# Experts in two groups of tokens with half tiles of 128 rows, and the scatters gathered behind the last attention unit

## What is computed

```python
x = _L0_conv_ref(x, ...)                      # softmax attention over 1024 positions, 4 images
t = _to_tokens(x)                             # (4, 1024, 128)
t = t + _L1_attn_ref(_ln_t(t), ...)
t = t + _L1_ffn_ref(_ln_t(t), ...)

def _L1_ffn_ref(x, Wg, bg, W1, b1, W2, b2):
    gate_logits = xf @ Wg + bg                # xf: (4096, 128), 8 experts
    top_w, top_i = jax.lax.top_k(gate_logits, 2)
    top_w = jax.nn.softmax(top_w, axis=-1)
    for e in range(E):
        h = jax.nn.gelu(xf @ W1[e] + b1[e], approximate=False)     # 512 hidden
        out = out + w_dense[:, e:e + 1] * (h @ W2[e] + b2[e])
```

## Time and profile before

| | us |
|---|---|
| median of 3 runs | 542.87 |
| lowest, highest | 540.98, 543.97 |
| profiled execution, its own time | 542.02 |
| its span, first to last instruction | 540.1 |
| TensorE busy | 397.8 (74%) |
| VectorE busy | 403.1 (75%) |
| GpSimd busy | 339.8 (63%) |
| ScalarE busy | 291.1 (54%) |

### The profile page before, as it was taken

The page is one execution under the profiler, slowest core; times in us unless marked ns, Lnnn a source line. Parts: engine busy times, 40 slices in busy tenths (PEclk is TensorE's granted clock), DMA queues, the critical chain, the costliest instruction groups (busy, mean ns, idle before and its releaser), DMA issues.

```text
span 540.1 us, 13443 instructions
## 1 busy us (share of the span) xinstructions
PE 397.8 (74%) x3902; PEld 294.2 (54%) x3903; DVE 403.1 (75%) x1119; ACT 291.1 (54%) x567; POOL 339.8 (63%) x361
## 2 busy tenths in 40 slices
PE   3767689999797998999884483001989898989336
PEld 2433356666575665666654362000778797979212
DVE  2578979988886878898878766700688898989457
ACT  3537887887675997776663123200545455555102
POOL 8000336567997558887599777773087878778800
PEclk9878999999998999999997597555899999999855
DMA  5730004200000000000620111332223323232176
GB/s 195 182 54 1 0 1 94 66 3 1 1 0 2 1 2 1 2 1 1 140 77 10 55 51 51 89 94 59 51 75 85 85 83 88 77 91 76 44 249 227
DMA packets 44244, 33.30 MB, mean 62 GB/s; under 512 B 17702, under 2 KB 37161, under 8 KB 44201
## 3 DMA queue, kind: packets, MB, share of 16 engines
q1 hardware_dynamic: 39594, 23.24, 17.1%
q0 software_dynamic: 4608, 9.51, 5.3%
HBM read 18.98 MB, written 13.73 MB: 61 GB/s over the span
## 4 chain that ended last, share of the span: by engine, by line
POOL 27%; PE 25%; DVE 20%; issue 17%; ACT 6%; DMA 3%; POOLq 0%; ACTq 0%; SPq 0%; DVEq 0%
POOL zbuf L503 12%; POOL ybuf L606 9%; PE PV L618 7%; PE SC L618 7%; PE MX L618 6%; DVE mx L1303 5%; PE PR L618 4%; DVE EL L1326 4%; POOL EL L544 2%; ACT EH L1032 2%; DVE TOK L1579 2%; ACT QK L950 2%; DVE QK L1271 1%; POOL carry L604 1%; DVE TOK L1584 1%
## 5 line engine op out<-in xcount | busy, mean ns | idle before, releaser
L544 POOL TENSOR_TENSOR EL<-E,EH 128x1024 f32 (+1 forms) x31 | 67.0, 2160 | 58.2 <-ACT EH L1032 58.2
L1031 ACT ACTIVATE E<-SC 128x512 f32<-128x512 f32 x128 | 77.2, 603 | 48.0 <-PE SC L618 34.1
L618 PE MATMUL PV<-VH,EH 128*128 128x129 f16 x512 | 97.2, 227 | 2.4 <-DVE TOK L1346 1.9
L606 POOL DMA_INDIRECT ybuf<-QK,yid x80 | 87.1, 1089 | 18.3 <-issue 12.5
L618 PE MATMUL SC<-QK 128*128 128x512 f16 x320 | 90.5, 386 | 9.9 <-ACT EH L1032 7.2
L618 PE MATMUL PV<-VH,EL 128*128 128x129 f16 x512 | 96.8, 224 | 0.0
L618 PE MATMUL PV<-VL,EH 128*128 128x128 f16 x512 | 96.7, 222 | 0.0
L1303 DVE TENSOR_REDUCE mx<-MX 128x1 f32<-128x1024 f32 x64 | 78.0, 1218 | 20.2 <-PE MX L618 19.9
L1032 ACT ACTIVATE EH<-SC 128x512 f32 (+1 forms) x128 | 77.5, 605 | 0.0
L503 POOL DMA_INDIRECT zbuf<-ZZ,posi x64 | 65.4, 1022 | 18.9 <-issue 18.9
L618 PE MATMUL MX<-EL,EH 128*128 x640 | 59.4, 246 | 1.6 <-DVE QK L1536 1.6
(11 more groups left out here) (200 smaller groups left out, 860.4 us busy)
## 6 DMA issues: line engine op xcount, KB each, us to landing
EH<-zbuf SPq DMA_DIRECT2D x40, 130.0 KB, 2.2
X<-in_x_dram SPq DMA_DIRECT2D x4, 512.0 KB, 5.1
zbuf<-zer SPq DMA_DIRECT2D x16, 128.0 KB, 3.3
X<-in_L_ffn_W_dram SPq DMA_DIRECT2D x1, 2048.0 KB
EL<-ybuf SPq DMA_DIRECT2D x4, 512.0 KB, 5.6
EH<-ybuf SPq DMA_DIRECT2D x4, 512.0 KB, 8.9
out_dram<-X SPq DMA_DIRECT2D x8, 256.0 KB, 2.7
ybuf<-QK,yid POOLq DMA_INDIRECT x80, 2.3
```

The lines of the kernel that those rows point to most:

```text
L544: nc.gpsimd.tensor_tensor(EL[:, w % 2, ds(i * 2, 2), c], E32h[1], EH[:, w % 2, ds(i * 2, 2), c], ALU.subtract).then_inc(e32_free[1], 1)
L606: nc.gpsimd.indirect_dma_start(out=ybuf, out_offset=bass.IndirectOffsetOnAxis(ap=yid[:, b, q:q + 1], axis=0), in_=y32[:, b, q, :], in_offs ...
L618: return nc.tensor.matmul(o, w, r, start=start, stop=stop)
L1031: nc.scalar.activation(E32h[h][:, p, :], SC[:, p, :], ACT.Exp, scale=sc)
```

## The change

- **Two groups.** Images 0 and 1 are group 0, images 2 and 3 group 1 (`G`, `GB`). Each has its own region in `zbuf` and its own tile table; `tile_table(0)` comes after the second image's `place`, `tile_table(1)` after the last. SyncE waits for a group's 32 scatters alone, then loads its 20 tiles; the pads of group 1 stand behind the load of tile 19 in its queue. TensorE's loop waits for both tables.
- **Half tiles.** A half tile has 128 rows (`TR`) and its own expert; two of them make a tile of the loop, still 256 rows, still 40 tiles. Loads are two to a tile. `hidden` and `output` run per half, with 128-column matmuls throughout: 24 and 26 instead of 12 and 16. b2 is added by one matmul a half (ones times a row of `B2`), which is prepared in the first steps by two DMAs, two ScalarE copies and one VectorE operation.
- **Output.** VectorE scales the sum once (128x256) and computes the row numbers in two small operations. Results have 20 buffers (`Y_BUFS`). The add on `carry` is gone.
- **First group combined in the second's loop.** Behind the load of tile 29 SyncE waits for all puts of group 0 and loads its outputs; VectorE mixes two token tiles with each of tiles 32 to 39. The tail has the 16 token tiles of group 1 left, and all transposes and stores.
- **Scatters.** None stands among the last unit's pairs. GpSimd's step of the last unit is the loop that other steps have; it makes the low half of the last pair (VectorE did), and then all 64 scatters.
- **ScalarE** makes all of the high halves (1024 columns). The loops of ScalarE, VectorE, GpSimd and SyncE are written out; TensorE's stays a `Fori`.

The diff, cut to its core:

```diff
@@ constants @@
-TR = 2 * P
-CAP = TT * P + TR
-NT = TT * P * 2 // TR + E
+G = 2
+GB = B // G
+TR = P
+DR = 2 * TR
+CAP = GB * S + TR
+SPAN = E * CAP + E * TR
+NH = GB * S * 2 // TR + E
+ND = NH // 2
+NT = G * ND
+Y_BUFS = ND
+MIX = 10
@@ block.sync @@
-            sp.wait_ge(table_ready, 2)
-            for e in range(E):
...
-            for h in range(2):
-                sp.wait_ge(scattered[h], 16 * T * B)
...
+            def load_tile(j):
+                b = j % IN_BUFS
+                if j >= IN_BUFS:
+                    sp.wait_ge(y_ready, j - IN_BUFS + 1)
+                for q in range(2):
+                    n = 2 * j + q
+                    r = sp.value_load(tabi[0:1, 0, n:n + 1], min_val=0, max_val=G * SPAN // TR - 1)
+                    sp.dma_start(tin[:, b, q], zbuf[ds(r * TR, TR), :]).then_inc(tin_full[b], 16)
...
+            for g in range(G):
+                pads(g)
+                sp.wait_ge(pad_done[g], 16 * 2 * E)
+                sp.wait_ge(table_ready, 3 * (g + 1))
+                sp.wait_ge(scattered[g], 16 * 2 * T * GB)
+                for j in range(ND * g, ND * (g + 1)):
+                    if j == ND + MIX:
+                        for b in range(Y_BUFS):
+                            sp.wait_ge(y_out[b], 32)
+                        for k in range(2 * GB):
+                            load_outputs(k)
+                    load_tile(j)
@@ block.gpsimd @@
-                if s >= UNITS or (u is None and a is None and before is None):
+                if s > UNITS or (u is None and a is None and before is None):
...
-                if s < UNITS - 1:
+                if s == UNITS:
+                    e_low(a, PAIRS - 1)
+                else:
...
-                else:
-                    for i in range(PAIRS):
-                        pair(i, (a, i - 1) if i else before)
-                        if i == 0:
-                            pool.wait_ge(rows_ready, 1)
-                        scatter(i)
-            for t in range(PAIRS, TT):
+            for t in range(TT):
                 if t % T == 0:
                     pool.wait_ge(rows_ready, t // T + 1)
                 scatter(t)
...
-                pool.wait_ge(carried, j4 + (b + 1))
-                nc.gpsimd.tensor_tensor(carry[:, 0:1], carry[:, 1:2], carry[:, 1:2], ALU.add).then_inc(carried, 1)
@@ block.tensor @@
-                for c in range(HC):
-                    o_ = WIDE[b % 2][:, c * TR:(c + 1) * TR]
-                    w = ds(e * HID + c * P, P)
-                    mm(o_, W1H[:, w], zT[:, b % 2, 0, :], True, False)
-                    mm(o_, W1H[:, w], zT[:, b % 2, 1, :], False, False)
-                    last = mm(o_, W1L[:, w], zT[:, b % 2, 0, :], False, True)
+                for q in range(2):
+                    e = expert(pe, tile_expert, 2 * b + q)
+                    r = slice(q * TR, (q + 1) * TR)
+                    for c in range(HC):
+                        o_ = WIDE[b % 2][:, c * DR + q * TR:c * DR + (q + 1) * TR]
+                        w = ds(e * HID + c * P, P)
+                        mm(o_, W1H[:, w], zT[:, b % 2, 0, r], True, False)
+                        mm(o_, W1H[:, w], zT[:, b % 2, 1, r], False, False)
+                        last = mm(o_, W1L[:, w], zT[:, b % 2, 0, r], False, True)
...
                 for q in range(2):
-                    o_ = MX[:, (b % 2) * HALF + q * TR:(b % 2) * HALF + (q + 1) * TR]
+                    e = expert(pe, last_experts if carried_over else tile_expert, 2 * (b % 2 if carried_over else b) + q)
+                    o_ = MX[:, (b % 2) * HALF + q * P:(b % 2) * HALF + (q + 1) * P]
+                    mm(o_, ones16[:], B2[:, ds(e * P, P)], True, False)
                     for c in range(HC):
...
+                        mm(o_, hh[:, b % 2, k], W2HL[:, g, 0, :], False, False)
+                        mm(o_, hh[:, b % 2, k], W2HL[:, g, 1, :], False, False)
+                        last = mm(o_, hl[:, b % 2, k], W2HL[:, g, 0, :], False, c == HC - 1)
...
-            pe.wait_ge(table_ready, 3)
+            pe.wait_ge(table_ready, 3 * G)
@@ block.scalar, in the first steps and in the loop @@
+                act.wait_ge(b2_in, 32)
+                for r in (0, 32):
+                    cp(B2[r:r + 1, :], B232[r:r + 1, :], WS).then_inc(b2_high, 1)
...
-                cp(hh[:, b % 2, HERE:], h32[:, b % 2, HERE:]).then_inc(hh_act_ready, 1)
+                cp(hh[:, b, :], h32[:, b, :]).then_inc(hh_ready, 1)
@@ block.vector @@
+                    if v == UNITS + GB - 1:
+                        tile_table(0)
...
-                nc.vector.tensor_copy(hh[:, b % 2, 0:HERE], h32[:, b % 2, 0:HERE]).then_inc(hh_ready, 1)
...
+                nc.vector.tensor_scalar(y32[:, b], sums, 1 / WS, None, ALU.mult).then_inc(y_ready, 1)
...
+            for j in range(NT):
+                low_halves(j)
+                if j + 2 < NT:
+                    rows_T(j + 2)
                 if j >= 2:
-                    output(j - 2, j - 2)
-                    output_low(j - 2, j - 2)
+                    output(j - 2)
+                k = j - (ND + MIX + 2)
+                if 0 <= k < T * GB // 2:
+                    mixes(range(4 * k, 4 * k + 4))
```

More of the change, by code:

```diff
@@ L364, in load_experts @@
             n = len(registers)
-            engine.load(registers, tabi[0:1, 1, ds(j, n)])
+            engine.load(registers, tabi[0:1, 1, ds(j * 2, n)])
         def expert(engine, registers, b):
@@ L442, in _, with pads @@
-            for b in range(IN_BUFS):
-                load_tile(b, b, None)
-            with sp.Fori(1, NT // IN_BUFS) as i:
-                for b in range(IN_BUFS):
-                    load_tile(i * IN_BUFS + b, b, i * 32)
-            for b in range(IN_BUFS):
-                sp.wait_ge(y_out[b], 32 * (NT // IN_BUFS))
+            def pads(g):
+                sp.wait_ge(table_ready, 3 * g + 1)
+                for e in range(E):
+                    low = g * SPAN + e * CAP
+                    r = sp.value_load(padrow[0:1, g, e:e + 1], min_val=low, max_val=low + GB * S)
+                    pad = zbuf[ds(r, TR), :]
+                    sp.dma_start(pad[:, 0:2 * P], zer[:, 0, :]).then_inc(pad_done[g], 16)
+                    sp.dma_start(pad[:, 2 * P:ROW], padid[:, 2 * g * E + e, :].bitcast(F16)).then_inc(pad_done[g], 16)
@@ L456, in _ @@
                 sp.dma_start(out[k // 2][:, c], X[:, k // 2, c]).then_inc(out_done, 16)
+            sp.wait_ge(pad_static, 16 * 2 * G)
+            for g in range(G):
+                pads(g)
[9 more added lines that the diff above has]
+                    load_tile(j)
+            for b in range(Y_BUFS):
+                sp.wait_ge(y_out[b], 32 * G)
+            for k in range(2 * GB, 2 * B):
+                load_outputs(k)
+            for k in range(2 * B):
+                store(k)
             sp.wait_ge(out_done, 16 * 2 * B)
@@ L608, in put @@
                         in_=y32[:, b, q, :], in_offset=None).then_inc(y_out[b], 16)
-            with pool.Fori(0, NT // IN_BUFS) as i:
-                for b in range(IN_BUFS):
-                    put(i * IN_BUFS, b)
+            for j in range(NT):
+                put(j)
         @block.tensor
@@ new lines, in rows_T, with low_halves, output @@
+                nc.vector.tensor_copy(zT[:, j % 2].rearrange("p h r -> p (h r)"), FT[j % 2]).then_inc(zt_ready, 1)
+            def low_halves(j):
+                b = j % 2
+                dve.wait_ge(hh_ready, j + 1)
+                if j >= 2:
+                    dve.wait_ge(y_full, j - 1)
+                nc.vector.tensor_tensor(hl[:, b, :], h32[:, b, :], hh[:, b, :], ALU.subtract).then_inc(hl_ready, 1)
+            def output(j):
+                b = j % Y_BUFS
+                if j >= Y_BUFS:
+                    dve.wait_ge(y_out[b], 32 * (j // Y_BUFS))
+                words = tin[:, j % IN_BUFS, :, 2 * P:ROW].bitcast(I32)
+                for q in range(2):
+                    n = 2 * j + q
+                    nc.vector.scalar_tensor_tensor(out=yid[:, b, q:q + 1], in0=words[:, q, 1:2],
+                                                   scalar=tabf[:, 1, n:n + 1], in1=words[:, q, 0:1],
+                                                   op0=ALU.not_equal, op1=ALU.add).then_inc(yid_ready, 1)
+                dve.wait_ge(y_full, j + 1)
+                dve.wait_ge(yid_ready, 2 * (j + 1))
+                sums = MX[:, (j % 2) * HALF:(j % 2) * HALF + DR].rearrange("p (q d) -> p q d", q=2)
+                nc.vector.tensor_scalar(y32[:, b], sums, 1 / WS, None, ALU.mult).then_inc(y_ready, 1)
@@ new lines, in mix @@
+            def mix(n):
+                t, half = divmod(n, 2)
+                if half == 0:
+                    if t % PAIRS == 0:
+                        dve.wait_ge(y_in[t // PAIRS], 16)
+                    src, w = yin[t // T][:, t % T, 0, :], WT[:, 0, t:t + 1]
+                else:
+                    src, w = yin[t // T][:, t % T, 1, :], WT[:, 1, t:t + 1]
+                    dve.wait_ge(mixed, t + 1)
```

(22 more changed lines are left out.)

273 lines of the change are left out of this document (95 added, 178 removed).

## The result

The changed kernel takes 602.67 us (median of 4 runs, 602.19 to 604.79) where the kernel before, on the same chip, takes 542.88 (540.98 to 543.97): 1.111 times the time, 95% interval 1.107 to 1.115. The profiled execution has a span of 600.1 us and a time of 602.19.

The account below looks back on a forecast made before the run. Three stages bound it: scatters (GpSimd), expert loop (TensorE), tail (VectorE). From a span of 540.1: -12.5 earlier start, +73.4 loop, -5.4 puts, -8.4 combination, +0.6 conversion; span 587.8, time 589.7 us, range 560 to 612.

Follow-up runs that it names:

- e1: The changed kernel with each half tile's weight addresses computed in one row of adds into registers, same 54 matmuls a tile: 545.82 us, 1.0054 times before.
- e4: e1 with TensorE's last two pairs of every attention step written out instead of looped: 541.85 us, 4.0 less than e1.
- e6: e1 with group 1's pads ahead of the first load, group 0's result loads behind the last tile's, its additions behind the last output: 549.02 us, 1.014.
- e7: e6 with b2's rows prepared by GpSimd and TensorE's last two attention pairs written out: 540.67 us, 0.996 of before.
- e9: e7 with VectorE waiting for the put of tile 37 before the first group's additions: 597.0 us beside 588.0 for the kernel before, on another chip.
- e10: e9 with the 128x512 copy of the transposed rows on ScalarE instead of VectorE: 618.0 us, on a chip where times scattered.
- e2: The kernel before, matmuls unchanged, with the expert's number taken from four register sets by turns so no address is shared: 613.68 us, 1.131 times before.
- e12: e7 with the first image's 16 scatters ahead of GpSimd's last low half and group 1's pads behind tile 7's load: 599.15 us beside 603.0.

## What to carry to other kernels

Before you cut matmuls of a dynamic loop in two, count the register instructions that their addresses need: here they took 0.12 to 0.14 us each (0.24 for two in the looped pairs, 4.86 for the 36 of a tile), 36 a tile set the pace at 4.86 us where the same matmuls with 10 of them take 3.01 (e1), and 14 cost nothing in a tile of 2.85. They show only as even gaps with nothing waited for (groups 0.24 us apart instead of 0.17). Where they do, write the loop out (0.17 instead of 0.23 us a group in e4) or compute the addresses in one row of adds ahead of the matmuls (3.01 instead of 4.86 us a tile in e1). When you scale a loop's time, take over the filling and the drain of its software pipeline as a term of its own. And before you speed up the engine that sets the pace, look at who comes next: GpSimd's puts were the bound in e1, and they became slower beside a faster loop.

## What the runs showed of the hardware

- GpSimd's indirect DMAs take longer beside some of VectorE's work: 0.97 us alone, 1.44 beside the low half and the other operations of a tile (e6), 6.3 to 6.5 beside 32 additions in a row (e6, e7, e9), though the first puts beside those additions take 0.97. Which of VectorE's operations does it is not settled; the 128x512 copy is not needed for it (1.79 us without it in e10).
- Six more register loads at a round's start lengthen its first distance by about 4.5 us, 0.75 each (e2).
- On two chips the kernel before took 8 and 11% longer, and the four kernels traced there (e9 to e12) have "issue" gaps on TensorE in the stretch of the scatters, 19 us in all in e9 and 40 in e10 between 270 and 366 us, where the first eight have at most two of 0.5 us. The cause is open.
